# Causal attention in one kernel with a mixture of experts: attention steps without a loop, and scores in array tiles of 64 by 64

## The chip, the cores and the metric

The kernel runs on one core of a Trainium2 chip. The metric is the device time of one launch in microseconds; lower is better. The matrix engine (TensorE, here PE), VectorE (DVE), ScalarE (ACT) and GpSimd (POOL) work in parallel, each through a list of instructions of its own; SyncE (SP) issues the DMA transfers. They wait for one another through semaphores only. Matmul results go to PSUM, eight banks of 128 partitions by 512 float32.

## The reference

Input x has 16 sequences of 512 rows and 128 channels. What the change touches is the first half, causal attention with 16 heads of 8 channels on a normalised x:

```python
q = x @ wq_lat @ wq_heads
k = x @ wk_lat @ wk_heads
v = x @ wv_lat @ wv_heads
...
att = jnp.einsum('bhqd,bhkd->bhqk', q, k) * SCALE
causal = jnp.tril(jnp.ones((Tx, Tx), dtype=bool))
att = jnp.where(causal[None, None], att, -jnp.inf)
att = jax.nn.softmax(att, axis=-1)
y = jnp.einsum('bhqk,bhkd->bhqd', att, v)
...
return y @ w_proj + b_proj
```

Behind it stand a layer norm and a residual, a shared feed-forward block and twelve experts, of which each row uses two. The change does not touch those.

## The kernel before

The attention works through 64 quads; a quad is four heads of one sequence. Each engine runs `step(gs, g)` for gs = -2 to 65, and `quad_steps` (L383 to L398) calls it: steps -2 to 3 and 56 to 65 are written out, steps 4 to 55 are a loop of 13 iterations of four steps. Inside the loop a semaphore is compared with a register (L394 to L396), which needs register instructions ahead of the wait; where two semaphores are waited for, `wait_apart` (L68) makes the wait an instruction of its own, which counts a semaphore `passed` up.

For a quad the scores are computed twice. `scores_by_query` (L1226 on, `most` in the step) has queries on PSUM partitions; DVE reduces them to row maxima (L1664, five units per quad). The maxima are negated, split on POOL into three bfloat16 parts, turned on PE (`turn_maxima`, L1276), copied by ACT (L968, `mT_sb`) and sent by SP (L555) as three further rows under the queries in `quad_area`. `scores_by_key` (L1250 on, `by_key`) then has keys on partitions and contracts over 64 rows, maxima included, so that ACT can apply the exponential straight from PSUM (L948); POOL zeroes what lies above the diagonal (L721), and PE multiplies with the values (`products`, L1308, four heads in column tiles of 32). `project` (L1220) makes the next queries and keys in even steps, which ACT copies (L935, L936), POOL splits into bfloat16 parts, and SP stores and loads again (L510, L503).

Two quads' rows lie on partitions 0 to 63 and 64 to 127, so that each score matmul uses half the rows of the array and all 128 columns (64x128), and two, `rg` 0 and 1, run side by side into two banks. PSUM has a ring of three such pairs of banks (RING = 3): an item of a step waits in `wait_emptied` (L1181 on) for the emptying of the item three before. The order in which PE issues is written out by hand in its `step` (L1352 on). An even step is by_key 1, most 3, project, most 4, products 2, turn_maxima, by_key 4, most 0, by_key 2, products 1 and 3, by_key 0, most 1, by_key 3, products 0, most 2. An odd step is by_key 1, most 2, products 0, by_key 2, most 4, products 1, by_key 4, most 0, turn_maxima, products 3, by_key 3, most 3, products 2, most 1, by_key 0, turn_back. SP's step loads a quad (L503, four transfers) before it sends the maxima (L555).

Units 0 and 1 of `most` hold the blocks on the diagonal of four query tiles. There the mask is added by two matmuls per bank (L1238) ahead of the scores, one for each half of the queries; `mask_to` and `mask_of` are built once, by fourteen selects in a chain on POOL (L694 to L702).

Of the kernel before, what the change touches and what calls it, by code (L numbers as in the profile page):

```python
# [5 lines left out]
ALU = mybir.AluOpType  # L6
# [3 lines left out]
BF16 = mybir.dt.bfloat16  # L10
# [57 lines left out]
def wait_apart(engine, sem, value, passed):  # L68

    engine.wait_ge(sem, value)  # L70
    engine.sem_inc(passed, 1)
# [109 lines left out]
def build(nc, a, out):  # L181
    with ExitStack() as ctx:
# [11 lines left out]
        mask_to = sb("mask_to", [P, 2, P], BF16)  # L194
        mask_of = sb("mask_of", [P, 2, ROWS], BF16)
# [279 lines left out]
        def _(sp):  # L475
# [99 lines left out]
            quad_steps(sp, step)  # L575
# [74 lines left out]
        def _(pool):  # L650
# [171 lines left out]
            quad_steps(pool, step)  # L822
# [40 lines left out]
        def _(act):  # L863
# [147 lines left out]
            quad_steps(act, step)  # L1011
# [106 lines left out]
        def _(pe):  # L1118
# [62 lines left out]
            def wait_emptied(gs, g, at):  # L1181
# [24 lines left out]
                masks = items(gs)[at][0] == "max" and items(gs)[at][1] < 2  # L1206
# [4 lines left out]
                if masks:  # L1211
                    wait_apart(pe, ready, done, s_passed)
                else:
                    pe.wait_ge(ready, done)
# [7 lines left out]
            def scores_by_query(gs, g, u, bank):  # L1222

                slot = (gs + 2) % 4
                if nth(MAX_ORDER, gs, u) == 0:
                    wait_apart(pe, s_qk[slot], 16 * (g + 2 - slot) + 64, s_passed)  # L1226

                def score(rg, head, at, qt, keys, first, closes):
                    return pe.matmul(ps[:, bank + rg, at:at + keys], rows(2 * rg + head, 0, qt * P, qt * P + P, slot, ROWS - 3),  # L1229
                                     rows(2 * rg + head, 1, first, first + keys, slot, ROWS - 3), start=closes is None, stop=closes is not False)  # L1230

                if u < 2:
                    for half in range(2):
                        for rg in range(2):
                            row = slice(ROWS * rg, ROWS * rg + ROWS)
                            keys = ps[:, bank + rg, :].rearrange("p (j k) -> p j k", k=P)[:, :, ROWS * half:ROWS * half + ROWS]
                            of = mask_of[row, half:half + 1].broadcast_to([ROWS, NT, ROWS])
                            pe.matmul(keys, mask_to[row, half], of, start=(half == 0), stop=False)  # L1238
                    for j, qt in enumerate(DIAGONALS):
                        for rg in range(2):  # L1240
                            last = score(rg, u, j * P, qt, P, qt * P, j == NT - 1)
                elif u < 4:
                    for at, qt, keys in ((0, 1, P), (P, 3, 3 * P)):
                        for rg in range(2):
                            last = score(rg, u - 2, at, qt, keys, 0, None)
                else:
                    for head in range(2):
                        for rg in range(2):
                            last = score(rg, head, 2 * P * head, 2, 2 * P, 0, None)
                last.then_inc(s_mx, 1)  # L1250

            def scores_by_key(gs, g, n, bank):

                slot = gs % 4
                if nth(EXP_ORDER, gs, n) == 0:
                    pe.wait_ge(s_m[slot], 8 * (g - slot) + 32)
                places = (((0, 0, 0),), ((0, 1, 0), (0, 3, 384)), ((1, 0, 0),), ((1, 1, 0), (1, 3, 384)), ((0, 2, 0), (1, 2, 256)))[n]
                for head, kb, at in places:
                    w = T - kb * P
                    for rg in range(2):  # L1260
                        last = pe.matmul(ps[:, bank + rg, at:at + w], rows(2 * rg + head, 1, kb * P, kb * P + P, slot, ROWS),  # L1261
                                         rows(2 * rg + head, 0, kb * P, T, slot, ROWS), start=True, stop=True)
# [165 lines left out]
            quad_steps(pe, step)  # L1428
# [136 lines left out]
        def _(dve):  # L1565
# [384 lines left out]
            quad_steps(dve, step)  # L1950
# [121 lines left out]
```

## Time and profile before

| | before |
|---|---|
| median of 3 runs | 1133.36 us (1133.0 to 1135.47) |
| profiled execution | 1131.17 us |
| its span | 1129.3 us |
| mean granted clock | 0.953 of full speed |
| PE busy | 992.2 us, 88% of the span |
| DVE busy | 853.1 us, 76% |
| ACT busy | 722.5 us, 64% |
| POOL busy | 632.7 us, 56% |

The span is what the profiler saw between the first and the last instruction; the profiled execution's time also has what lies around it. Busy shares are means over stages: the attention with its start takes about the first half, the experts most of the rest. Matmul ends are modelled, and overlapping matmuls make PE look fuller than its array is. A line such as `ACT pT_area L948 <- PE ps L1261` in the view of the waits says that ACT's instruction of L948 sat idle until PE's of L1261 released it; in a timeline the same stands in brackets.

### The profile page before, as it was taken

How to read it: one execution, taken by the hardware profiler on the slowest of the kernel's cores; microseconds unless marked ns; L12 is line 12 of the kernel's file. 1: busy time of each engine (PE TensorE's matmuls, PEld its weight loads, DVE VectorE, ACT ScalarE, POOL GpSimd, SP SyncE). 2: the span in 40 equal slices, each digit the busy share in tenths (PEclk: the TensorE clock that was granted, in tenths of full speed). 3: DMA queues.
4: the chain of work that ended last, by engine and by line, in shares of the span. 5: the costliest groups of instructions: out<-in, count | busy, mean ns of one | idle time of the engine just before them, and what ended most of it. 6: DMA issues, size and time to landing. Idle time of an engine off the chain costs nothing. (4 is left out here: it accounts for less than half of the span.)

```text
span 1129.3 us, 31995 instructions
## 1 busy us (share of the span) xinstructions
PE 992.2 (88%) x8685; PEld 618.6 (55%) x8685; DVE 853.1 (76%) x2487; ACT 722.5 (64%) x1234; POOL 632.7 (56%) x1195
## 2 busy tenths in 40 slices
PE   4589999999999999978879998759999999998774
PEld 2553344443444434433456665339999888897532
DVE  5678888888888888877689985327777777777646
ACT  4578788888888888866646665316565555556426
POOL 4327777777777777755217777742444444444344
PEclk9889999999999999999959998969999999999988
DMA  8413333333333333343251111122222222221176
GB/s 221 104 31 104 112 104 109 113 106 106 105 107 113 113 110 104 107 115 103 74 214 57 54 54 56 51 80 60 61 66 67 60 65 67 63 61 57 32 252 197
DMA packets 135726, 108.21 MB, mean 96 GB/s; under 512 B 32207, under 2 KB 127866, under 8 KB 135658
## 3 DMA queue, kind: packets, MB, share of 16 engines
q1 hardware_dynamic: 124842, 88.19, 27.8%
q0 software_dynamic: 8544, 17.78, 4.4%
q10 hardware_dynamic: 2272, 1.45, 0.5%
q8 instruction: 28, 0.46, 0.2%
q14 instruction: 40, 0.33, 0.1%
HBM read 56.70 MB, written 50.68 MB: 95 GB/s over the span
## 5 line engine op out<-in xcount | busy, mean ns | idle before, releaser
L1664 DVE TENSOR_REDUCE maxima<-ps 128x8 f32<-128x1024 f32 x320 | 380.4, 1222 | 76.7 <-PE ps L1229 69.8
L948 ACT ACTIVATE pT_area<-ps 128x1024 f32<-128x1024 f32 x320 | 320.8, 1023 | 86.2 <-PE ps L1261 80.9
L843 POOL DMA_INDIRECT ys_dram<-quad_area,place_cur x139 | 133.1, 958 | 188.2 <-issue 126.5
L721 POOL TENSOR_SCALAR_AFFINE_SELECT pT_area<-pT_area 128x256 f32<-128x256 f32 (+1 forms) x448 | 186.6, 439 | 90.8 <-ACT pT_area L948 88.3
L1308 PE MATMUL ps<-pT_area,quad_area 128*32 128x512 f32 (+3 forms) x2048 | 185.5, 446 | 0.6 <-POOL pT_area L721 0.6
L833 POOL DMA_INDIRECT xs_dram<-quad_area,idx_cur x128 | 123.1, 961 | 74.6 <-issue 73.7
L1261 PE MATMUL ps<-quad_area 64*128 64x256 bf16 (+3 forms) x1024 | 125.9, 301 | 30.7 <-DMA quad_area<-mT_sb 28.1
L1991 DVE SCALAR_TENSOR_TENSOR quad_area<-ps,be_cur,xnT 128x256 f32<-128x256 f32 (+1 forms) x228 | 92.0, 456 | 61.5 <-PE ps L1541 28.0
L1530 PE MATMUL ps<-quad_area 128*128 128x256 f32 (+1 forms) x456 | 130.3, 368 | 7.0 <-DVE quad_area L1991 6.8
L1096 ACT ACTIVATE xnT<-ps,be_cur 128x256 f32<-128x256 f32 (+1 forms) x228 | 103.1, 453 | 49.2 <-PE ps L1531 48.1
L1229 PE MATMUL ps<-quad_area 61*128 61x128 bf16 (+2 forms) x1792 | 127.0, 241 | 4.7 <-ACT pT_area L948 2.7
L1531 PE MATMUL ps<-quad_area 128*128 128x256 f32 (+1 forms) x456 | 128.0, 362 | 0.0
L1541 PE MATMUL ps<-outT_area,quad_area 128*128 128x128 f32 x834 | 107.8, 278 | 2.7 <-DVE quad_area L2009 2.3
L1541 PEld LDWEIGHTS ps<-outT_area,quad_area 128*128 128x128 f32 x834 | 102.4, 192 | 10.8 <-issue 5.5
L1229 PEld LDWEIGHTS ps<-quad_area 61*128 61x128 bf16 x1792 | 70.1, 94 | 68.8 <-ACT pT_area L948 50.2
L1261 PEld LDWEIGHTS ps<-quad_area 64*128 64x128 bf16 x1024 | 38.4, 94 | 104.9 <-DVE maxima L1664 65.9
L1531 PEld LDWEIGHTS ps<-quad_area 128*128 128x128 f32 x456 | 84.2, 191 | 10.0
L1530 PEld LDWEIGHTS ps<-quad_area 128*128 128x128 f32 x456 | 78.5, 191 | 17.5 <-DVE quad_area L1991 11.0
L1085 ACT ACTIVATE quad_area<-ps 128x256 f32<-128x256 f32 (+1 forms) x76 | 27.7, 365 | 80.3 <-PE ps L1516 80.3
L1308 PEld LDWEIGHTS ps<-pT_area,quad_area 128*32 128x32 f32 x2048 | 43.7, 108 | 57.8 <-issue 48.0
L1081 ACT ACTIVATE quad_area<-pT_area 128x768 f32 x76 | 63.4, 835 | 0.1
L1238 PE MATMUL ps<-mask_of,mask_to 64*128 64x256 bf16 x512 | 50.8, 273 | 5.9 <-DVE maxima L1664 4.8
(234 smaller groups left out, 1501.9 us busy)
## 6 DMA issues: line engine op xcount, KB each, us to landing
qk_dram<-split_area SPq DMA_DIRECT2D x192, 128.0 KB, 2.3
quad_area<-qk_dram SPq DMA_DIRECT2D x256, 96.0 KB, 2.3
row_area<-xs_dram SPq DMA_DIRECT2D x63, 132.0 KB, 2.1
pT_area<-ys_dram SPq DMA_DIRECT2D x16, 512.0 KB, 5.0
pT_area<-in_L_ffn_We SPq DMA_DIRECT2D x12, 384.0 KB, 6.3
out_dram<-pT_area SPq DMA_DIRECT2D x7, 512.0 KB, 3.0
xs_dram<-row_area SPq DMA_DIRECT2D x5, 528.0 KB, 4.4
split_area<-in_L_ffn_We SPq DMA_DIRECT2D x12, 192.0 KB, 3.8
```

The lines of the kernel that those rows point to most:

```text
L721: return pool.affine_select(out=blocks, in_=blocks, compare_op=ALU.is_ge, fill=0.0, base=0, pattern=[[0, count], [1, P]], channel_multipli ...
L833: pool.indirect_dma_start(xs_dram, at, rows_cur[:, b % DEPTH, t, :], None).then_inc(s_scat[par], 16)
L843: pool.indirect_dma_start(ys_dram, at, ys[:, ns % 2, h, :], None).then_inc(s_yst[ns % 2], 16)
L948: act.activation(pT[:, gs % 2, n, :], ps[:, bank:bank + 2, :].rearrange("p a b -> p (a b)"), ACT.Exp).then_inc(s_exp, 1)
L1096: act.activation(gelE[:, ring, 0:width(ns)], ps[:, ring, 0:width(ns)], ACT.Gelu, bias=be_cur[:, ns % 8, 3 + k:4 + k]).then_inc(s_ge, 1)
L1229: return pe.matmul(ps[:, bank + rg, at:at + keys], rows(2 * rg + head, 0, qt * P, qt * P + P, slot, ROWS - 3), rows(2 * rg + head, 1, firs ...
L1261: last = pe.matmul(ps[:, bank + rg, at:at + w], rows(2 * rg + head, 1, kb * P, kb * P + P, slot, ROWS), rows(2 * rg + head, 0, kb * P, T, ...
L1308: last = pe.matmul(ps[32 * i:32 * i + 32, bank, kb * P:T], v_cur[:, slot, kb, i, :], pT[:, buf, n, 512 * rg + at:512 * rg + at + w], start ...
L1530: pe.matmul(ps[:, ring, 0:w], w1_cur[:, par, HR + k * P:HR + (k + 1) * P], xsT[:, par, 0:w], start=True, stop=True)
L1531: pe.matmul(ps[:, ring, RT:RT + w], w1_cur[:, par, k * P:(k + 1) * P], xsT[:, par, 0:w], start=True, stop=True).then_inc(s_he, 1)
L1541: last = pe.matmul(ps[:, Y_BANKS[par], h * C:(h + 1) * C], hidT[:, par, k, h * P:(h + 1) * P], w2_cur[:, par, k * C:(k + 1) * C], start=(k ...
L1664: dve.tensor_reduce(to, ps[:, bank:bank + 2, :].rearrange("p a (j k) -> p a j k", k=P), AX, ALU.max).then_inc(s_mxf, 1)
```

## The change

The change has four parts. `quad_steps` now calls every step from -2 to 65 with constants, so all 64 quads are written out on each engine, and `wait_apart` with a constant adds no count, so that the wait sits on the instruction behind it. All scores are computed in tiles of 64 rows by 64 columns: each matmul of 128 queries (or keys) becomes two of 64, which write partitions 0 to 63 and 64 to 127 of the same bank, so that four run where two ran. In units 0 and 1 one mask matmul per tile, after the scores, covers the later 64 keys of each block. The earlier 64 are all allowed, which needs another choice of keys: the first 64 queries of a tile take the 64 keys before their own block in place of the later half of it, and where there are none (the first tile) key 0 is scored 64 times. And POOL builds the smaller masks with four selects in place of fourteen.

```diff
 def wait_apart(engine, sem, value, passed):
     engine.wait_ge(sem, value)
-    engine.sem_inc(passed, 1)
+    if not isinstance(value, int):
+        engine.sem_inc(passed, 1)
...
-        def quad_steps(engine, step):
-            for g in range(FIRST, 4):
-                step(g, g)
-            with engine.Fori(1, B - EARLY) as it:
-                for q in range(4):
-                    step(4 + q, 4 * it + q)
-            for g in range(4 * (B - EARLY), LAST + 1):
+        def quad_steps(step):
+            for g in range(FIRST, LAST + 1):
                 step(g, g)
...
-                for half in range(2):
-                    same = to[:, half, ROWS * half:ROWS * half + ROWS]
-                    chain(pool.affine_select(out=same, in_=same, compare_op=ALU.not_equal, fill=1.0, base=0,
-                                             pattern=[[-1, ROWS]], channel_multiplier=1))
-                    chain(pool.affine_select(out=of[:, half], in_=of[:, half], compare_op=ALU.is_ge, fill=MASKED, base=0,
-                                             pattern=[[-1, ROWS]], channel_multiplier=1))
-                for late, value in ((to[:, 1, ROWS:], 0.0), (to[:, 1, 0:ROWS], 1.0), (of[:, 1], MASKED)):
-                    chain(pool.affine_select(out=late, in_=late, compare_op=ALU.not_equal, fill=value, base=1 - ROWS,
-                                             pattern=[[0, ROWS]], channel_multiplier=1))
+                chain(pool.affine_select(out=to, in_=to, compare_op=ALU.not_equal, fill=1.0, base=0,
+                                         pattern=[[-1, ROWS]], channel_multiplier=1))
+                chain(pool.affine_select(out=of[:, 0], in_=of[:, 0], compare_op=ALU.is_ge, fill=MASKED, base=0,
+                                         pattern=[[-1, ROWS]], channel_multiplier=1))
...
+                def half(rg, later, head, qt, at, keys, first, last=False):
+                    lo = qt * P + ROWS * later
+                    return pe.matmul(ps[ROWS * later:ROWS * later + ROWS, bank + rg, at:at + keys.shape[-1]],
+                                     rows(2 * rg + head, 0, lo, lo + ROWS, slot, ROWS - 3), keys, start=first, stop=last)
...
                 if u < 2:
-                    for half in range(2):
-                        for rg in range(2):
-                            row = slice(ROWS * rg, ROWS * rg + ROWS)
-                            keys = ps[:, bank + rg, :].rearrange("p (j k) -> p j k", k=P)[:, :, ROWS * half:ROWS * half + ROWS]
-                            of = mask_of[row, half:half + 1].broadcast_to([ROWS, NT, ROWS])
-                            pe.matmul(keys, mask_to[row, half], of, start=(half == 0), stop=False)
-                    for j, qt in enumerate(DIAGONALS):
-                        for rg in range(2):
-                            last = score(rg, u, j * P, qt, P, qt * P, j == NT - 1)
+                    for j, qt in enumerate(DIAGONALS):
+                        for rg in range(2):
+                            if qt == 0:
+                                half(rg, 0, u, qt, j * P + ROWS, key_rows(rg, u, 0, ROWS), True)
+                            else:
+                                half(rg, 0, u, qt, j * P, key_rows(rg, u, qt * P - ROWS, qt * P + ROWS), False)
+                        for rg in range(2):
+                            half(rg, 1, u, qt, j * P, key_rows(rg, u, qt * P, qt * P + P), qt == 0)
+                        if qt == 0:
+                            for rg in range(2):
+                                half(rg, 0, u, qt, j * P, key_rows(rg, u, 0, 1).broadcast_to([ROWS - 3, ROWS]), False)
+                    for later in range(2):
+                        for rg in range(2):
+                            row = slice(ROWS * rg, ROWS * rg + ROWS)
+                            late_keys = ps[ROWS * later:ROWS * later + ROWS, bank + rg, :].rearrange("p (j k) -> p j k", k=P)[:, :, ROWS:]
+                            last = pe.matmul(late_keys, mask_to[row], mask_of[row].broadcast_to([ROWS, NT, ROWS]), start=False, stop=True)
...
                     w = T - kb * P
-                    for rg in range(2):
-                        last = pe.matmul(ps[:, bank + rg, at:at + w], rows(2 * rg + head, 1, kb * P, kb * P + P, slot, ROWS),
-                                         rows(2 * rg + head, 0, kb * P, T, slot, ROWS), start=True, stop=True)
+                    for later in range(2):
+                        lo = kb * P + ROWS * later
+                        for rg in range(2):
+                            last = pe.matmul(ps[ROWS * later:ROWS * later + ROWS, bank + rg, at:at + w],
+                                             rows(2 * rg + head, 1, lo, lo + ROWS, slot, ROWS),
+                                             rows(2 * rg + head, 0, kb * P, T, slot, ROWS), start=True, stop=True)
```

The other units of `most` are split in the same way. The first place where the order of instructions moves is PE at the beginning of an even step (`by_key` 1, `most` 3, `project`, `most` 4, `products` 2). Before, inside the loop; the last figures of a row are the output's partitions and columns, or its shape:

```order
L1214 REGISTER_ALU
L1261 MATMUL ps<-quad_area 128x384 [waits m_loaded2,maxima_taken]
L1261 MATMUL ps<-quad_area 128x384
L1261 MATMUL ps<-quad_area 128x128 x2
L1214 REGISTER_ALU
L70 ISA [waits maxima_taken]
L1229 MATMUL ps<-quad_area 128x128 [waits qk_loaded0]
L1229 MATMUL ps<-quad_area 128x128
L1229 MATMUL ps<-quad_area 128x384 x2
L1220 MATMUL ps<-y_sb,w_qkv 128x512 [waits exp_done]
```

With the change (`by_key` is L1263, `most` L1217, `project` L1207):

```order
L1263 MATMUL ps<-quad_area 64x384 [waits m_loaded2,maxima_taken]
L1263 MATMUL ps<-quad_area 64x384 x3
L1263 MATMUL ps<-quad_area 64x128 x4
L1217 MATMUL ps<-quad_area 64x128 [waits qk_loaded0,maxima_taken]
L1217 MATMUL ps<-quad_area 64x128 x3
L1217 MATMUL ps<-quad_area 64x384 x4
L1207 MATMUL ps<-y_sb,w_qkv 128x512 [waits exp_done]
```

The three register and count instructions are gone, both waits of `most` sit on its first matmul, and each group has twice the matmuls. The second place is a unit with masks, in the same step (`most` 0, then `by_key` 2). Before:

```order
L1238 MATMUL ps<-mask_of,mask_to 128x4x64 [waits part1_ready]
L1238 MATMUL ps<-mask_of,mask_to 128x4x64 x3
L1229 MATMUL ps<-quad_area 128x128 x8
L1214 REGISTER_ALU
L1261 MATMUL ps<-quad_area 128x512 [waits maxima_taken]
L1261 MATMUL ps<-quad_area 128x512
```

With the change:

```order
L1217 MATMUL ps<-quad_area 64x64 [waits part1_ready]
L1217 MATMUL ps<-quad_area 64x64
L1217 MATMUL ps<-quad_area 64x128 x2
L1217 MATMUL ps<-quad_area 64x64 x2
L1217 MATMUL ps<-quad_area 64x128 x12
L1239 MATMUL ps<-mask_of,mask_to 64x4x64 x4
L1263 MATMUL ps<-quad_area 64x512 [waits maxima_taken]
L1263 MATMUL ps<-quad_area 64x512 x3
```

Twelve matmuls become 22, and the masks stand behind the scores. The third place is POOL's setup with the change, where before the pair of L696 and L698 stood four times and L701 six times ahead of the casts:

```order
L690 AFFINE_SELECT mask_to<-mask_to 64x64
L692 AFFINE_SELECT mask_of<-mask_of 64x64 [waits pool_step]
L690 AFFINE_SELECT mask_to<-mask_to 64x64 [waits pool_step]
L692 AFFINE_SELECT mask_of<-mask_of 64x64 [waits pool_step]
L694 CAST before_bf<-before 128x128 [waits pool_step]
L695 CAST ident_bf<-ident 128x128
L174 TENSOR_TENSOR pT_area<-pT_area,minus_half 128x8 [waits ln_root_steps] x2
```

The last row is the inverse root of the first normalisation (L173 before), which now has four selects ahead of it.

## Rows read from the trace of the kernel before

**Rows 1.** Window; busy us (count) of PE, PEld, DVE, ACT, POOL; clock, DMA share

```profile
100.00:450.00 350.00, 330.89 (x4163) 140.99 (x4159) 303.75 (x356) 282.57 (x356) 252.39 (x639) 1.00 0.38 108
```

**Rows 2.** Waits, 100 to 450 us: us in total, times, longest us

```profile
PE ps L1261 <- DMA quad_area<-mT_sb: 18.6, 24, 1.2
```

**Rows 3.** Timeline, PE, written-out steps: start us, duration us, line, operation, count [idle before]

```profile
83.89 0.24 PE L1276 MATMUL ps<-ident_bf,m_part 128*48 128x128 bf16 x1
...
87.53 0.39 PE L1261 MATMUL ps<-quad_area 64*128 64x384 bf16 x4 [1.17 <-DVE maxima L1664]
87.75 0.40 PE L1229 MATMUL ps<-quad_area 61*128 61x128 bf16 x4
88.07 1.12 PE L1220 MATMUL ps<-y_sb,w_qkv 128*128 128x512 f32 x2
...
90.02 0.24 PE L1276 MATMUL ps<-ident_bf,m_part 128*48 128x128 bf16 x1
...
98.23 0.24 PE L1276 MATMUL ps<-ident_bf,m_part 128*48 128x128 bf16 x1
```

**Rows 4.** The same view of PE, steps inside the loop

```profile
201.99 0.24 PE L1276 MATMUL ps<-ident_bf,m_part 128*48 128x128 bf16 x1
...
203.62 0.28 PE L1238 MATMUL ps<-mask_of,mask_to 64*128 64x256 bf16 x2
...
205.94 0.40 PE L1261 MATMUL ps<-quad_area 64*128 64x384 bf16 x4 [0.90 <-DMA quad_area<-mT_sb]
206.28 0.40 PE L1229 MATMUL ps<-quad_area 61*128 61x128 bf16 x4
...
208.55 0.24 PE L1276 MATMUL ps<-ident_bf,m_part 128*48 128x128 bf16 x1
...
216.83 0.24 PE L1276 MATMUL ps<-ident_bf,m_part 128*48 128x128 bf16 x1
...
223.10 0.24 PE L1276 MATMUL ps<-ident_bf,m_part 128*48 128x128 bf16 x1
...
231.54 0.24 PE L1276 MATMUL ps<-ident_bf,m_part 128*48 128x128 bf16 x1
```

**Rows 5.** The same view, ACT and then SP, same steps

```profile
201.61 1.02 ACT L948 ACTIVATE pT_area<-ps 128x1024 f32<-128x1024 f32 x1 [0.32 <-PE ps L1261]
202.53 0.26 ACT L968 ACTIVATE mT_sb<-ps 48x128 bf16<-48x128 bf16 x1
...
201.06 1.87 SPq L503 DMA_DIRECT2D quad_area<-qk_dram  x4
202.98 1.61 SPq L555 DMA_DIRECT2D quad_area<-mT_sb  x2
```

**Rows 6.** The same view of PE, an even step's unit with masks, and products

```profile
211.02 0.39 PE L1238 MATMUL ps<-mask_of,mask_to 64*128 64x256 bf16 x4
211.24 0.40 PE L1229 MATMUL ps<-quad_area 61*128 61x128 bf16 x8
211.46 0.40 PE L1261 MATMUL ps<-quad_area 64*128 64x384 bf16 x4
...
213.60 1.07 PE L1308 MATMUL ps<-pT_area,quad_area 128*32 128x512 f32 x8
```

**Rows 7.** Groups by form, weight loads, 100 to 450 us: busy us, mean ns

```profile
L1261 PEld LDWEIGHTS ps<-quad_area 64*128 64x128 bf16 x758 | 28.5, 94 | 70.2 <-DVE maxima L1664 47.5 <-DMA quad_area<-mT_sb 10.3 <-issue 9.3
```

**Rows 8.** Timeline of the start, POOL, then DVE

```profile
6.94 0.23 POOL L696 TENSOR_SCALAR_AFFINE_SELECT mask_to<-mask_to 64x64 bf16<-64x64 bf16 x1
...
11.70 0.24 POOL L701 TENSOR_SCALAR_AFFINE_SELECT mask_of<-mask_of 64x64 bf16<-64x64 bf16 x1
...
12.49 1.68 POOL L173 TENSOR_TENSOR pT_area<-pT_area,minus_half 128x8 f32<-128x8 f32 x1
...
14.21 0.17 DVE L1596 SCALAR_TENSOR_TENSOR pT_area<-pT_area 128x8 f32<-128x8 f32 x1 [6.63 <-POOL pT_area L173]
```

**Rows 9.** DMA queues, 80 to 135 us: packets, MB, share of 16 engines

```profile
q8 instruction: 6, 0.10, 0.8%
```

More of the change, by code:

```diff
@@ L193, in build @@
         ident_bf = sb("ident_bf", [P, P], BF16)
-        mask_to = sb("mask_to", [P, 2, P], BF16)
-        mask_of = sb("mask_of", [P, 2, ROWS], BF16)
+        mask_to = sb("mask_to", [P, ROWS], BF16)
+        mask_of = sb("mask_of", [P, 1, ROWS], BF16)
         ysum = kept_xT = y_sb
@@ L573, in step @@
                     store_late(4 * g + (EARLY - 1) * HEADS, 1, 2)
-            quad_steps(sp, step)
+            quad_steps(step)
             sp.wait_ge(s_st, 5 * QUADS)
@@ L820, in step @@
                     split_rows(gs, g, 2)
-            quad_steps(pool, step)
+            quad_steps(step)
             def scatter(ns, n):
@@ L1009, in copy_yT @@
                 act.activation(yT[:, ns % 2, :], ps[:, YT_TURN, :], ACT.Copy).then_inc(s_yTsb, 1)
-            quad_steps(act, step)
+            quad_steps(step)
             act.wait_ge(s_w2, 160)
@@ L1205, in wait_emptied @@
                 quad = g - back + AHEAD[kind]
-                masks = items(gs)[at][0] == "max" and items(gs)[at][1] < 2
                 if kind == "max":
@@ L1210, in wait_emptied @@
                     ready, done = s_exp, UNITS * quad + nth(EXP_ORDER, gs - back, u) + 1
[L1211 to L1214, printed above, removed]
+                wait_apart(pe, ready, done, s_passed)
             def project(gs, g, s, bank):
@@ new lines, in key_rows @@
+                def key_rows(rg, head, first, last):
+                    return rows(2 * rg + head, 1, first, last, slot, ROWS - 3)
+                if u < 2:
+                    for j, qt in enumerate(DIAGONALS):
[10 more added lines that the diff above has]
+                    for later in range(2):
@@ L1242, in scores_by_query @@
+                            last = pe.matmul(late_keys, mask_to[row], mask_of[row].broadcast_to([ROWS, NT, ROWS]), start=False, stop=True)
                 elif u < 4:
                     for at, qt, keys in ((0, 1, P), (P, 3, 3 * P)):
-                        for rg in range(2):
-                            last = score(rg, u - 2, at, qt, keys, 0, None)
+                        for later in range(2):
+                            for rg in range(2):
+                                last = half(rg, later, u - 2, qt, at, key_rows(rg, u - 2, 0, keys), True, True)
@@ L1246, in scores_by_query @@
                 else:
                     for head in range(2):
-                        for rg in range(2):
-                            last = score(rg, head, 2 * P * head, 2, 2 * P, 0, None)
+                        for later in range(2):
+                            for rg in range(2):
+                                last = half(rg, later, head, 2, 2 * P * head, key_rows(rg, head, 0, 2 * P), True, True)
                 last.then_inc(s_mx, 1)
@@ L1255, in scores_by_key @@
                 if nth(EXP_ORDER, gs, n) == 0:
-                    pe.wait_ge(s_m[slot], 8 * (g - slot) + 32)
+                    wait_apart(pe, s_m[slot], 8 * (g - slot) + 32, s_passed)
                 places = (((0, 0, 0),), ((0, 1, 0), (0, 3, 384)), ((1, 0, 0),), ((1, 1, 0), (1, 3, 384)), ((0, 2, 0), (1, 2, 256)))[n]
@@ L1259, in scores_by_key @@
                     w = T - kb * P
-                    for rg in range(2):
-                        last = pe.matmul(ps[:, bank + rg, at:at + w], rows(2 * rg + head, 1, kb * P, kb * P + P, slot, ROWS),
-                                         rows(2 * rg + head, 0, kb * P, T, slot, ROWS), start=True, stop=True)
+                    for later in range(2):
+                        lo = kb * P + ROWS * later
+                        for rg in range(2):
+                            last = pe.matmul(ps[ROWS * later:ROWS * later + ROWS, bank + rg, at:at + w],
+                                             rows(2 * rg + head, 1, lo, lo + ROWS, slot, ROWS),
+                                             rows(2 * rg + head, 0, kb * P, T, slot, ROWS), start=True, stop=True)
                 last.then_inc(s_st, 1)
@@ L1426, in project_y @@
                 last.then_inc(s_proj, 1)
-            quad_steps(pe, step)
+            quad_steps(step)
             pe.wait_ge(s_exp, UNITS * QUADS)
@@ L1948, in shared @@
                     tile_table()
-            quad_steps(dve, step)
+            quad_steps(step)
             dve.wait_ge(s_vcur, QUADS)
```

3 lines of the change are left out of this document (removed).

## Prediction, made before the changed kernel was run

> **What bounds the kernel now.** I read the windows first [rows 1]. In the steady part of the attention TensorE (PE) is busy for 330.89 us of 350, DVE for 303.75, ACT for 282.57, POOL for 252.39, all at a granted clock of 1.00, the 2.4 GHz level. PE is nearest to full, yet its busy share is inflated by overlapping matmuls, so I asked next for the waits [rows 2]: the reader is to see that PE waits at L1261 for the rows of maxima (`quad_area<-mT_sb`) 24 times, 18.6 us in all. The timeline gives the beat: in the looped steps the starts of `turn_maxima` (L1276) are 6.56, 8.28, 6.27 and 8.44 us apart [rows 4], so four quads take 29.55 us and two take 14.78; 350 / 14.78 = 23.7, one such wait per two quads, always at an even step. So each two quads are one loop: maxima turned on PE (201.99), copied by ACT (202.53), sent by SP (202.98), landed and first used by PE at 205.94 [rows 4, 5]; then the even step's scores, exponentials and maxima lead to the odd step's `turn_maxima`, after which it starts again. DVE needs at least 303.75 / 23.7 = 12.8 us per two quads, PE something over that; neither fills the 14.78. What counts is latency along this loop.
>
> **What leaving the loop gives.** `before` already holds written-out steps with constant waits: quads 2 to 4 stand 6.13 and 8.21 us apart (83.89, 90.02, 98.23), 14.34 for two [rows 3]. The same two places in the looped steps (201.99, 208.55, 216.83) take 14.84 [rows 4]. So constants are worth 0.50 here. It can be seen where: the first scores by key to the next group is 205.94 to 206.28, 0.34 us, in the loop, and 87.53 to 87.75, 0.22, written out, because separate register and count instructions stood between; and from `turn_maxima` to those scores it is 3.95 against 3.64. For the other two places (6.27 + 8.44 = 14.71 looped [rows 4]) no undisturbed written-out row exists. At least nothing is gained there, at most they also fall to 14.34, 0.37. I take 0.25, nearer the upper end, since the 8.44 contains a delay of SP's that partly stays: four loads of L503 from 201.06 on, after waits, stand ahead of the L555 that sends the maxima [rows 5], and the change leaves that order as it is. Per iteration 0.50 + 0.25 = 0.75; 13 iterations give **-9.8 us** (bounds -6.5 and -11.3). The six written-out pairs of steps gain nothing from this.
>
> **What the shorter masks give.** A mask and its scores in one unit take 211.02 to 211.46, 0.44 us, half for the four masks, half for the eight scores [rows 6]. Each row half streams 2 x 256 mask columns and 4 x 128 score columns, 1,024. Now each of four tiles streams 512 score columns and 256 of mask, 768, a quarter less: 0.11 us, if the four run side by side. Two units per quad, 128 in all, would make 14.1 us. But only what lies on the loop counts. The odd step's two are covered: behind the one (203.62) PE waits 0.90 us at 205.94 in any case [rows 4], and an earlier end of the other, just ahead of the turn at 201.99, helps nobody, since ACT cannot copy the turned maxima before its exponential begun at 201.61 ends, at 202.53 [rows 5]. Of the even step's two I count one, so 0.11 x 32 pairs = **-3.5 us** (bounds 0 and -14.1).
>
> **What tiles of 64 by 64 cost.** The number of score matmuls and masks per quad goes from 52 to 100, and of weight loads as well. The trace of before has no tile of 64 by 64. The nearest rows are the products of L1308: eight matmuls in column tiles of 32, 512 columns each, take 1.07 us from 213.60 on [rows 6], while two matmuls of 512 columns in the same type over the whole array take 1.12 [rows 3]. So four column tiles do run side by side, and eight weight loads cost nothing in view: bound below, 0. The upper bound: a load of a score group takes 94 ns [rows 7]; if each group's two further loads stood wholly in view, that is 0.19 us, on some six groups of the loop per pair, 0.19 x 6 x 32 = +36 us. I take 0.02 per group, close to the products' nothing, because only the first four loads of a group have no matmul of their own shape to hide behind: 0.02 x 6 x 32 = **+3.8 us**. The Trainium skill ("TensorEngine Tiling (Array Packing)", Restrictions and Instruction Overhead) speaks against the change: column tiling switches its fast weight load off, and each matmul costs some 60 cycles whatever its width. By that rule a unit of 22 matmuls would take, as an estimate, 22 x 25 ns = 0.55 us and not 0.33, and the sum would be about 7 us higher. The products' rows, column-tiled and not slowed by their loads, do not bear the first half out; no row here decides the second.
>
> **What the shorter setup gives.** Fourteen chained selects run on POOL from 6.94 to the casts; the first inverse root (L173) starts behind them at 12.49, and DVE idles 6.63 us until 14.21 for it [rows 8], with the whole normalisation behind. Ten selects go. The chain from 6.94 to the last select at 11.70 is thirteen steps, 0.37 each, so ten are 3.7 us. DVE would still wait 2.9 us, so its own work does not take over. I take **-3.7 us** (bounds 0, if the loads of x or weights are late next, and -3.8).
>
> **Instruction fetch.** Between 80 and 135 us, half of it written out, the instruction queue moved 6 packets [rows 9]. Written out throughout, the attention fetches them all along; its cover is that the DMA engines are a little over a third busy (0.38, [rows 1]). I cost it at nothing; without cover it is a rival.
>
> **Sum.** -9.8 - 3.5 + 3.8 - 3.7 = -13.2. The profiled execution took 1131.17; 1118.0 comes out. The median of the runs is 1133.36, 2.2 higher, so I predict 1120.2 us.
>
> **Rivals.**
> *PE itself is the bound*, and every mask saving counts. For it: 330.89 of 350 busy [rows 1]. Against: the 18.6 us of waits for transfers [rows 2], which no busy engine would have. All four units of a pair then count, -14.1 in place of -3.5, and the time is about 1110.
> *Another wait takes over.* When PE comes sooner, the ring of three pairs of banks, DVE at 12.8 us per pair, or SP's queue sets the beat. For it: DVE's busy share, and SP's loads ahead of L555 [rows 5]. Then half the loop's saving stays and masks and tiles matter no more; -3.7 - 4.9 leaves about 1125.
> *Slower: small tiles pay per instruction.* A unit of 12 matmuls takes 0.44 us now [rows 6], 0.037 each. If that were a price per instruction and not of the columns, 22 cost 0.81, +0.37 on the one unit of the loop, and the other five groups of eight cost 0.29, some 0.05 more than the narrow ones now: +0.37 + 0.25 = 0.62 per pair, 32 pairs +20 in place of -3.5 + 3.8, and the time is about 1140. Its place is the score groups of the even step; it makes the kernel slower than before from 0.42 us per pair on, where it eats the other 13.5 (9.8 + 3.7). The rule of the skill's page on tiling named above is this mechanism in a milder form; by its 0.55 us the time stays below before's.
> *The change does nothing*, since fetched instructions delay the maxima's transfers as much as the constants save: 16 KB packets on the engine that carries a row of maxima, 0.4 us per pair in the mean. For it: the 6 packets in 55 us [rows 9]. Against: those very steps ran at 14.34 per pair [rows 3]. Then about 1131 to 1134.
>
> **How the numbers follow.** Forecast 0.60, PE bound 0.14, another wait 0.12, slower tiles 0.09, nothing 0.05. The forecast's own range, from the bounds of the terms (loop -6.5 to -11.3, masks 0 to -7, tiles 0 to +8), is 1112 to 1127. The range that holds 8 in 10 takes in both faster rivals: 1108 to 1130. A measurement of this kernel can tell some 0.2%, 2.3 us, from no change. Faster by more: 0.60 + 0.14 + 0.12 = 0.86; slower 0.09; the same 0.05.
>
> **What would show it.** Right: starts of `turn_maxima` 14.2 to 14.4 us apart per two quads in all steps; scores after the first group by key 0.22 behind it; a mask group followed by the next unit 0.33 to 0.36 after its first score; the first inverse root at 8.7 us; a wait for `mT_sb` still once per pair. Wrong: a unit of over 0.44 us, weight loads on the timeline between tiles of a group, the pair's beat at 14.7 or above, or more than one instruction packet near each late transfer.

## Result and profile after

The changed kernel took 1116.3 us (median of 4 runs, 1115.21 to 1117.18), the kernel before 1134.34 beside it. The ratio is 0.9848 with a 95% interval of 0.983 to 0.9865, 17.2 us less (the two medians differ by 18.0). The forecast was 1120.2 in a range of 1108 to 1130. The profiled execution took 1117.18 us, its span 1115.4, 13.9 less than before's. Runs of one kernel scatter by several microseconds, and the granted clock goes with it in the main: of 30 further runs of the kernel before, the three with a mean granted clock of 0.956 took 1127.7 to 1128.7 us and the three with 0.946 took 1135.7 to 1139.1, though the one with 0.957 took 1134.2.

The windows of the steady attention, with the columns of [rows 1]:

```profile
100.00:450.00 350.00, 330.96 (x6597) 144.34 (x6595) 310.05 (x363) 291.51 (x366) 258.39 (x654) 1.00 0.41 114
```

PE has 6,597 matmuls in place of 4,163 and is busy for the same 331 us; DVE and ACT do 2 to 3% more in the same stretch, which is the progress. The waits of PE for the maxima, and of ACT for PE, in the same stretch:

```profile
ACT pT_area L939 <- PE ps L1263: 48.6, 121, 1.2
...
PE ps L1263 <- DVE maxima L1667: 14.6, 19, 0.8
...
PE ps L1263 <- DMA quad_area<-mT_sb: 4.4, 5, 1.3
```

The wait at the even step's first group is still there once per two quads ([rows 2]: 24 times, 18.6 us; now 19 + 5 times, 19.0 us), only that most are now put down to DVE's reductions, which end at nearly the same moment. The timeline of PE over two quads, to be held beside [rows 4] and [rows 6], then SP and DVE:

```profile
196.06 0.24 PE L1279 MATMUL ps<-ident_bf,m_part 128*48 128x128 bf16 x1
...
199.94 0.41 PE L1263 MATMUL ps<-quad_area 64*64 64x384 bf16 x8 [0.77 <-DVE maxima L1667]
200.16 0.42 PE L1217 MATMUL ps<-quad_area 61*64 61x128 bf16 x8
200.50 1.12 PE L1207 MATMUL ps<-y_sb,w_qkv 128*128 128x512 f32 x2
201.56 0.41 PE L1217 MATMUL ps<-quad_area 61*64 61x256 bf16 x8
201.90 0.64 PE L1311 MATMUL ps<-pT_area,quad_area 128*32 128x256 f32 x8
202.47 0.24 PE L1279 MATMUL ps<-ident_bf,m_part 128*48 128x128 bf16 x1
...
204.88 0.40 PE L1217 MATMUL ps<-quad_area 61*64 61x64 bf16 x18
205.12 0.28 PE L1239 MATMUL ps<-mask_of,mask_to 64*64 64x256 bf16 x4
205.23 0.38 PE L1263 MATMUL ps<-quad_area 64*64 64x384 bf16 x8
...
210.46 0.24 PE L1279 MATMUL ps<-ident_bf,m_part 128*48 128x128 bf16 x1
...
197.05 1.57 SPq L551 DMA_DIRECT2D quad_area<-mT_sb  x2
...
195.20 4.61 DVE L1667 TENSOR_REDUCE maxima<-ps 128x8 f32<-128x1024 f32 x4
```

The turns of the maxima stand 6.41 and 7.99 us apart, 14.40 for two quads in place of 14.71 and 14.84. The first score group is followed after 0.22 (0.34 in the loop before). A unit with masks now takes 204.88 to 205.23, 0.35 us and not 0.44, so four tiles do run side by side. But a group of eight small matmuls ahead of another shape takes 0.34 (200.16 to 200.50, 201.56 to 201.90), where four wide ones took 0.32 (87.75 to 88.07 [rows 3]). The rows of SP and DVE show what the wait is for: DVE's reductions end at 199.81, and PE's group starts at 199.94, 1.32 us after SP has issued both transfers of the maxima (198.62). Before it was 1.35 after them (204.59 to 205.94 [rows 4, 5]), so the transfer still comes last, by about 0.1 us; experiment 4 tests this.

The start, POOL and DVE, as in [rows 8]:

```profile
6.71 0.23 POOL L690 TENSOR_SCALAR_AFFINE_SELECT mask_to<-mask_to 64x64 bf16<-64x64 bf16 x1
...
8.63 1.68 POOL L174 TENSOR_TENSOR pT_area<-pT_area,minus_half 128x8 f32<-128x8 f32 x1
...
10.35 0.17 DVE L1599 SCALAR_TENSOR_TENSOR pT_area<-pT_area 128x8 f32<-128x8 f32 x1 [2.62 <-POOL pT_area L174]
```

The inverse root is 3.86 us earlier, and DVE waits 2.62 in place of 6.63. The larger of the two instruction queues moved 86 packets of 16 KB in the whole span, against 28.

Between the turns of quads 4 and 56, which holds the former loop, the two traces differ by 9.4 us (98.23 to 482.75, now 95.12 to 470.28). Of the other 4.5 us by which the spans differ, 3.1 lie ahead of quad 4's turn and 3.4 in the experts, while the end of the attention and the shared block behind it take 3.1 us longer; the last stage gives back 1.1. The gain in the experts has no term in the forecast.

### The profile page after: what moved, and what is told of

The parts are those of the page before. It is cut to its first block, busy times and chain, and to the rows that moved or that the text cites. A ratio compares the mean times of both kernels' runs of the same rounds, so it can differ in the third digit from the quotient of the medians.

```text
span 1115.4 us, 34300 instructions
## 1 busy us (share of the span) xinstructions
PE 985.2 (88%) x11757; PEld 619.1 (56%) x11757; DVE 851.2 (76%) x2487; ACT 722.9 (65%) x1234; POOL 630.8 (57%) x1185
## 4 chain that ended last, share of the span: by engine, by line
PE 24%; DMA 7%; DVE 7%; POOL 6%; issue 5%; DVEq 1%; ACT 1%; ACTq 1%; SPq 0%; POOLq 0%
POOL xs_dram L824 6%; DMA ys_dram<-quad_area,place_cur 5%; PE ps L1533 5%; PE ps L1534 5%; PE ps L1544 5%; PE ps L1559 1%; DMA xs_dram<-quad_area,idx_cur 1%; PE ps L1519 1%; DVEq L1988 1%; PE ps L1443 1%; PE ps L1562 1%; PE ps L1427 1%; PE ps L1563 1%; PE ps L1441 1%; PE ps L1565 1%
## 5 line engine op out<-in xcount | busy, mean ns | idle before, releaser
L1263 PE MATMUL ps<-quad_area 64*64 64x384 bf16 (+3 forms) x2048 | 130.6, 309 | 30.8 <-DVE maxima L1667 17.3
L1217 PE MATMUL ps<-quad_area 61*64 61x128 bf16 (+3 forms) x3840 | 131.4, 240 | 11.0 <-DVE maxima L1667 6.4
L1217 PEld LDWEIGHTS ps<-quad_area 61*64 61x64 bf16 x3840 | 71.2, 107 | 93.4 <-ACT pT_area L939 62.3
L1263 PEld LDWEIGHTS ps<-quad_area 64*64 64x64 bf16 x2048 | 46.5, 105 | 107.2 <-DVE maxima L1667 81.0
L1443 PE MATMUL ps<-y_sb,ws 128*128 128x512 f32 x64 | 39.8, 709 | 14.9 <-DVE v_all L1822 14.7
```

What stands on the lines that cost most here:

```text
L1217: return pe.matmul(ps[ROWS * later:ROWS * later + ROWS, bank + rg, at:at + keys.shape[-1]], rows(2 * rg + head, 0, lo, lo + ROWS, slot, RO ...
L1263: last = pe.matmul(ps[ROWS * later:ROWS * later + ROWS, bank + rg, at:at + w], rows(2 * rg + head, 1, lo, lo + ROWS, slot, ROWS), rows(2 * ...
```

## Experiments

Each was a variant of the kernel before or of the changed one. What is compared is the time, and in the trace the beat, the distance of the starts of `turn_maxima` over two quads. It is given as the median of the 26 pairs between quads 4 and 56 (as the mean where the loop is kept, since its two places differ). In the four traces that have the changed kernel's attention it is 14.40 to within 0.002 us, so it tells a tenth of a microsecond that the time alone can't.

**1. Only written out.** The kernel before with two edits: old tiles, masks and setup.

```diff
-    engine.sem_inc(passed, 1)
+    if not isinstance(value, int):
+        engine.sem_inc(passed, 1)
...
-            with engine.Fori(1, B - EARLY) as it:
...
+            for g in range(FIRST, LAST + 1):
                 step(g, g)
```

> The kernel before with all steps written out and nothing else: old tiles, old masks, old setup. Theory (the beat of two quads is a loop of waits, and register waits lengthen it): turn_maxima 14.3 to 14.5 us apart per two quads in all steps, from 14.78; 9 to 11 us faster than before, about 1123 to 1125. Rival (matrix engine full, so the gain is the masks' and tiles'): 14.6 to 14.8, at most 3 us faster.

Measured: 1114.52 us (1110.74 to 1116.46), ratio 0.9811 (0.9788 to 0.9833). PE's turns:

```profile
193.94 0.24 PE L1272 MATMUL ps<-ident_bf,m_part 128*48 128x128 bf16 x1
...
200.22 0.24 PE L1272 MATMUL ps<-ident_bf,m_part 128*48 128x128 bf16 x1
...
208.30 0.24 PE L1272 MATMUL ps<-ident_bf,m_part 128*48 128x128 bf16 x1
```

6.28 and 8.08 here, and 14.334 for two quads over all: the theory's beat, and below the changed kernel's 14.40. So the whole gain of the loop comes from writing it out, and tiles and masks together take 0.07 per two quads back. The written-out steps of before, at 14.34, still had the counts of `wait_apart`, and experiment 1 has none; so on this loop the counts cost nothing that can be seen, and the register waits, or whatever else the loop form brings, cost all of it. The time, though, is some 9 us below the theory's 1123 to 1125. In this one trace 4.6 us are gained ahead of quad 4's turn, although the old setup is still there, and 4.1 in the experts (experiments 9 and 10, and the last section).

**2. Ten selects put back** into the changed kernel's setup.

```diff
+                for _ in range(5):
+                    chain(pool.affine_select(out=to, in_=to, compare_op=ALU.not_equal, fill=1.0, base=0,
+                                             pattern=[[-1, ROWS]], channel_multiplier=1))
```

> The changed kernel with ten redundant selects put back into the setup's chain. Theory: the first inverse root at 12.4 us in place of 8.6, the first turn_maxima 2.7 to 3.8 us later, the beat untouched at 14.40, the time 2.7 to 3.8 us over the changed kernel's (about 1119 to 1120). Rival (the start waits for loads anyway): the first turn_maxima under 1 us later, 1116 to 1117.

Measured: 1119.52 us (1117.93 to 1120.74), 3.2 over the changed kernel; beat 14.40; the inverse root at 12.82. DVE's first reduction of maxima came at 48.37, against 45.01 in the changed kernel and 48.10 in the kernel before. The shorter setup is worth 3.1 to 3.4 us at this place and 3.2 in the time, as the theory has it; experiment 8 does not bear it out.

**3. Wide tiles but for the masked units**, in the changed kernel.

```diff
-                        for later in range(2):
-                            for rg in range(2):
-                                last = half(rg, later, u - 2, qt, at, key_rows(rg, u - 2, 0, keys), True, True)
+                        for rg in range(2):
+                            last = whole(rg, u - 2, at, qt, keys)
...
```

> The changed kernel with 64 by 64 tiles in the units with masks only; the other scores in tiles of 64 by 128 as before. Theory (a group of small tiles costs some 0.02 us more): the beat falls from 14.40 to about 14.3, 2 to 4 us faster than the changed kernel. Rival A (small tiles pay per matmul): 14.1 or less, 10 us or more faster. Rival B (small tiles are free, a change of tile shape costs): 14.4 to 14.6, the same time or up to 6 us slower.

Measured: 1121.57 us (1118.4 to 1123.18), beat 14.57. Rival B holds. PE around a masked unit:

```profile
204.34 0.39 PE L1263 MATMUL ps<-quad_area 64*128 64x512 bf16 x2
204.66 0.42 PE L1217 MATMUL ps<-quad_area 61*64 61x64 bf16 x18
204.91 0.28 PE L1243 MATMUL ps<-mask_of,mask_to 64*64 64x256 bf16 x4
205.12 0.39 PE L1263 MATMUL ps<-quad_area 64*128 64x384 bf16 x4
...
205.44 1.06 PE L1310 MATMUL ps<-pT_area,quad_area 128*32 128x512 f32 x8
```

The wide group is followed by the small one after 0.32, where a group of one shape follows after 0.22 to 0.24, and the unit takes 0.46 in place of 0.35: about 0.1 us at each change of tile shape. Small tiles in the masks alone therefore lose: the beat is 14.57, for 14.334 with wide tiles and the old masks (experiment 1) and 14.40 with small tiles in all scores.

**4. The odd step's turn earlier**, in the changed kernel.

```diff
+                    copy_max_rows(gs, g)
                     probabilities(gs, g, 4)
-                    copy_max_rows(gs, g)
...
+                    turn_maxima(gs, g)
                     by_key(gs, g, 4)
                     most(gs, g, 0)
-                    turn_maxima(gs, g)
```

> The changed kernel with odd steps' turn_maxima two groups earlier on TensorE (ahead of by_key 4 and most 0) and its copy ahead of ScalarE's exponential 4. Theory (the beat runs through that copy, which stands behind exponential 4): the transfer starts about 1 us earlier, and the beat falls by 0.2 to 0.3, to where DVE's reductions of the odd step free the banks: 14.1 to 14.2, 6 to 9 us faster than the changed kernel. Rival (TensorE or DVE is full, the wait for the maxima only follows): 14.4, no faster.

Measured: 1115.89 us (1111.36 to 1119.45), beat 14.30. PE, then DVE:

```profile
197.38 0.41 PE L1263 MATMUL ps<-quad_area 64*64 64x384 bf16 x8 [0.15 <-DMA quad_area<-mT_sb]
197.86 0.41 PE L1217 MATMUL ps<-quad_area 61*64 61x128 bf16 x8
...
193.00 4.81 DVE L1667 TENSOR_REDUCE maxima<-ps 128x8 f32<-128x1024 f32 x4
```

PE's wait for the maxima falls from 0.77 to 0.15, and the next group now stands 0.48 behind it in place of 0.22: it waits for DVE's four reductions, which end at 197.8. So the transfer was on the loop, by 0.10 us; behind it stands DVE. The direction is the theory's, the size is a third to a half of it, and in the time nothing of it can be seen: 1115.89 for 1116.3, where the theory had 6 to 9 us.

**5. The changed kernel again**, without an edit.

> The changed kernel once more, beside the next three. All theories: 1114 to 1118 us, turn_maxima 14.40 us apart per two quads; its waits for late maxima of over 1 us, one or two in the attention, need not fall on the same quads (if they come from fetched instructions, they may; if by chance, they won't).

Measured: 1116.19 us (1112.58 to 1117.55), ratio 0.9841 (0.9818 to 0.9863); beat 14.40. The change's first trace has one turn late by 0.57 (quad 43), this one turns late by 0.07 and 0.12 on other quads. What makes them late stays open: in the first, one packet of each of the two instruction queues moved during the wait, but in experiment 11 a turn was 1.1 late with no instruction packet near it.

**6 and 7. More masks.** In the changed kernel the mask products of a unit are issued more than once; 6 doubles them in all steps, 7 triples them in even ones.

```diff
+                    times = 2 if gs >= 0 else 1
+                    for again in range(times):
+                        for later in range(2):
...
+                                last = pe.matmul(late_keys, mask_to[row], mask_of[row].broadcast_to([ROWS, NT, ROWS]), start=False, stop=again == times - 1)
```

> The changed kernel with each mask product of the steps 0 on issued twice, so that a unit streams as many columns per tile as before the change (masked scores are then lower still; the probabilities are the same). Theory after the first four runs (all four units of two quads lie behind ScalarE's exponentials or the maxima's copy, so the shorter masks gave nothing): the beat stays at 14.40 to 14.42, the time within 1 us of the changed kernel. Rival A (one unit per two quads counts, as the forecast had it): 14.51, 3.5 us slower. Rival B (TensorE is full): 14.83, 14 us slower.

> The changed kernel with the mask products of even steps issued three times, 0.21 us more in each of the two units. Theory (these units have 0.2 to 0.4 us of slack against ScalarE's four exponentials in a row): the beat 14.40 to 14.50. Rival A (one of the two units counts in full): 14.61. Rival B (both count): 14.82.

Measured: 6 took 1119.82 us (1116.25 to 1121.42), 7 1127.61 in a single run. Turns of 6, then of 7:

```profile
195.23 0.24 PE L1281 MATMUL ps<-ident_bf,m_part 128*48 128x128 bf16 x1
...
201.53 0.24 PE L1281 MATMUL ps<-ident_bf,m_part 128*48 128x128 bf16 x1
...
209.69 0.24 PE L1281 MATMUL ps<-ident_bf,m_part 128*48 128x128 bf16 x1
```

```profile
198.61 0.24 PE L1281 MATMUL ps<-ident_bf,m_part 128*48 128x128 bf16 x1
...
205.01 0.24 PE L1281 MATMUL ps<-ident_bf,m_part 128*48 128x128 bf16 x1
...
213.29 0.24 PE L1281 MATMUL ps<-ident_bf,m_part 128*48 128x128 bf16 x1
```

14.46 and 14.68 here, 14.468 and 14.686 over all. Both theories missed. One reading fits both runs: the even step's two units lie one behind the other ahead of ACT's exponentials, with some 0.14 us of slack together, so that 0.21 more costs 0.07 and 0.43 more costs 0.29. What the slack is against was not tried by itself. The kernel of run 6 streams as many columns per tile as before the change; so the shorter masks are worth 14.468 - 14.400 = 0.068 per two quads, 2.2 us over 32 pairs, and small tiles with the old amount of columns are 14.468 - 14.334 = 0.134 above run 1, 4.3 us.

**8. Old tiles, the earlier turn, and the selects behind the second inverse root**, all on top of experiment 1.

```diff
                 inverse_root(pool, rstd1[:, tiles], root1[:, 0, tiles], minus_half).then_inc(s_pow1, 1)
+                if k == 1:
+                    build_masks()
```

> All steps written out with the old tiles and masks (the first run), and two things more: odd steps' turn_maxima and its copy earlier, and the fourteen selects behind the second inverse root. Theory (constants and setup are worth their time, tiles nothing): the beat 14.20 to 14.25, the first inverse root at about 7.5 us, 1108 to 1111 us, faster than every other version. Rival (with the old tiles the earlier turn gives nothing, since DVE ends last): 14.33, 1110 to 1114.

Measured: 1113.65 us (1112.5 to 1117.48), ratio 0.9829 (0.9806 to 0.9851); beat 14.31, inverse root at 7.91, first reduction at 45.14. The rival's beat, nearly: with old tiles DVE ends as late as the transfer. Its time can't be told from experiment 1's, and hardly from the changed kernel's; the 1108 to 1111 us of the theory were missed. DVE's first reduction comes 2.7 us earlier than in experiment 1 (47.84), and the time has 0.9 of it.

**9 and 10. The counts in the experts.** 9 is the kernel before with the new `wait_apart` alone. 10 is the changed kernel with the old, counting wait in the experts' steps (on DVE, POOL and SP).

```diff
-                    wait_apart(dve, s_yst[ns % 2], stored(ns - 8, n - 8), s_passed)
+                    wait_counted(dve, s_yst[ns % 2], stored(ns - 8, n - 8), s_passed)
...
-                wait_apart(dve, s_b2c, n + 1, s_passed)
-                wait_apart(dve, s_wt, 4 * n + 4, s_passed)
+                wait_counted(dve, s_b2c, n + 1, s_passed)
+                wait_counted(dve, s_wt, 4 * n + 4, s_passed)
...
```

> The kernel before with the new wait_apart alone (constants are not counted); loop, tiles, masks and setup as before. Theory (the experts' written-out last steps, where each count stands ahead of a DVE instruction, are a gain that the forecast overlooked): looped quads at 14.78 per two as before; the experts' stage, first row turn to first sum, 306 us in place of 310; 4 to 5 us faster than before. Rival (the 310 us of before's trace was chance): the stage as before or scattered, the time within 1.5 us of before's.

> The changed kernel with the old, counting wait in the experts' steps (DVE, POOL and SP) only. Theory: the stage takes 310 us again, 4 us slower than the changed kernel, about 1120; the attention's beat 14.40. Rival: 306 and 1116.

Measured: 9 took 1124.08 us (1122.97 to 1125.51), ratio 0.9916 (0.9888 to 0.9945), beat 14.78. 10 took 1119.68 us (1118.62 to 1121.69), 3.4 over the changed kernel, beat 14.40. From the first row turn of the experts to the first sum it is 310.1 us before, 304.6 in 9, 308.9 in 10, and 306.7 and 305.7 in the changed kernel's two traces. DVE in the last, written-out expert steps, before the change:

```profile
1045.31 0.21 DVE L1971 SCALAR_TENSOR_TENSOR weight_other<-row_area,be_cur 128x1 f32<-128x1 f32 x1
1045.67 0.16 DVE L1974 TENSOR_TENSOR weight_cur<-weight_cur,weight_other 128x1 f32<-128x1 f32 x1
1046.40 0.87 DVE L1991 SCALAR_TENSOR_TENSOR quad_area<-ps,be_cur,xnT 128x128 f32<-128x128 f32 x3 [0.57 <-issue]
...
1049.57 0.87 DVE L1991 SCALAR_TENSOR_TENSOR quad_area<-ps,be_cur,xnT 128x128 f32<-128x128 f32 x3 [0.57 <-issue]
```

The same of 9:

```profile
1041.92 0.21 DVE L1972 SCALAR_TENSOR_TENSOR weight_other<-row_area,be_cur 128x1 f32<-128x1 f32 x1
1042.16 0.16 DVE L1975 TENSOR_TENSOR weight_cur<-weight_cur,weight_other 128x1 f32<-128x1 f32 x1
1042.88 0.87 DVE L1992 SCALAR_TENSOR_TENSOR quad_area<-ps,be_cur,xnT 128x128 f32<-128x128 f32 x3 [0.56 <-PE ps L1542]
...
1045.82 0.87 DVE L1992 SCALAR_TENSOR_TENSOR quad_area<-ps,be_cur,xnT 128x128 f32<-128x128 f32 x3 [0.56 <-PE ps L1542]
```

And of 10:

```profile
1040.51 0.21 DVE L1980 SCALAR_TENSOR_TENSOR weight_other<-row_area,be_cur 128x1 f32<-128x1 f32 x1
1040.87 0.16 DVE L1983 TENSOR_TENSOR weight_cur<-weight_cur,weight_other 128x1 f32<-128x1 f32 x1
1041.60 0.87 DVE L2000 SCALAR_TENSOR_TENSOR quad_area<-ps,be_cur,xnT 128x128 f32<-128x128 f32 x3 [0.57 <-issue]
```

From `weight_other` to the sum that waits for it it is 0.36 with the count and 0.24 without, 0.12 each, twice per step (the second place is the product behind the sum with the bias); a step takes 3.17 with and 2.94 without. Over the last twelve steps, from one `weight_cur` sum to the next, it is 39.1 us before and 38.8 in 10, against 36.1 in 9 and 35.9 in both traces of the changed kernel: 2.9 us either way. This is shown from both sides, by undoing and by doing it alone. The 5.5 us of the stage in 9 is more than these steps explain, and of the 9.8 us of its median the stage is little more than half (its profiled execution, 1125.51, is 5.7 below before's). The rest stays open, beside a scatter of before's runs of several microseconds. The shared block between attention and experts calls `wait_apart` too (L1898, L1903), in steps that were written out already; from the last turn to the first row turn it takes 218.4 us before and 217.7 to 220.3 in the other traces, so nothing can be seen of its counts.

**11. The odd step's masks three times.** The edit is that of 7, for odd steps in place of even ones.

> The changed kernel with the mask products of odd steps issued three times, 0.21 us more in each of these two units. Theory (these units lie behind the maxima's copy and the transfer): the beat 14.40 to 14.45. Rival (TensorE is full): 14.83.

Measured: 1119.52 us in a single run; the turns, 14.40 for two quads although these units stream 0.43 us more:

```profile
197.21 0.24 PE L1281 MATMUL ps<-ident_bf,m_part 128*48 128x128 bf16 x1
...
203.40 0.24 PE L1281 MATMUL ps<-ident_bf,m_part 128*48 128x128 bf16 x1
...
211.61 0.24 PE L1281 MATMUL ps<-ident_bf,m_part 128*48 128x128 bf16 x1
```

So PE is not the bound, and the odd step's units are covered.

## Why the prediction was right, and where it was not

The sum of -13.2 us was meant for five terms and came near the measured 17.2; its parts stand so. That it came so near is in part luck: a missed term and a loop term taken too small (together 5.4 us) stand against three terms that were too favourable (2.4 us).

- *What bounds the kernel.* Right: a loop of waits, not a full engine. Experiment 11 gives PE 0.43 us more work per two quads and the beat stays; experiment 4 sends the maxima earlier and the beat falls.
- *Leaving the loop, -9.8.* Right in kind and short, by more than its bound of -11.3 allows. Experiment 1 has 14.334 per two quads, the value of the written-out steps that the trace of before already held (14.34 [rows 3]); over the 26 pairs between quads 4 and 56 that is 372.7 us for 384.5, -11.8. Of the "register and count instructions" to which the prediction put the 0.50, the counts have no part: those written-out steps had them. The step that was too careful is the second pair of places, 0.25 taken for the 8.44: it fell to 8.08, so SP's loads ahead of the transfer did not hold it.
- *Shorter masks, -3.5.* Right that the odd units count for nothing (11). The even step's two count together behind 0.14 us of slack, so the term is -2.2 (6 and 7), not one whole unit.
- *Tiles of 64 by 64, +3.8.* Right in size: +4.3, 0.134 per two quads (6 against 1), with some 0.02 us per group ahead of another shape (0.34 for 0.32). The 0.02 was picked between 0 and 0.19, near the end to which the products pointed, so that it fits so closely is luck; its reason, loads with no matmul to hide behind, was not tried. The weight loads grew from 94 ns [rows 7] to between 104 and 107. The rival of a price per instruction fell: a unit of 22 matmuls takes 0.35 us, and the rival had 0.81. With it fell the estimate of 0.55 us that the prediction drew from the Trainium skill, page "TensorEngine Tiling (Array Packing)" (Instruction Overhead): the overhead of some 60 cycles that the page states for each matmul does not add up over matmuls in different tiles. No run here shows what one such matmul alone takes.
- *Shorter setup, -3.7.* Nearly right: DVE's first reduction is 3.1 us earlier (45.01 for 48.10), and putting the selects back costs 3.2 us of time (2). But taking them out of the way of the old tiles left 0.9 us of time (8 against 1), so it is shown from one side only.
- *Instruction fetch, 0.* Right as far as it can be seen: experiment 1 has the beat of the few steps that were written out before. Single late transfers remain, under 1 us in all in the changed kernel.
- *What was missed.* The forecast took `wait_apart` for a matter of the attention. It is used in the experts too, whose first and last steps were written out already; there the count goes, which shortens the last twelve steps by 2.9 us, and to undo it costs 3.4 us of time (9 and 10). So the sentence ahead of the prediction that the change does not touch the experts is wrong. No rival had this. Of the rivals, only "another wait takes over" had some truth: DVE stands 0.1 us behind the transfer (4, 8), but it took nothing from the constants.
- *The range.* The bounds that the prediction names for its own range give 1111 to 1131, not 1112 to 1127 (at the slow end -6.5 + 0 + 8 - 3.7 = -2.2), and those of masks and tiles are narrower there than in their paragraphs, with no reason given. The wider range of 1108 to 1130 holds either way.

With the measured sizes: -11.8 - 2.2 + 4.3 - 3.1 - 3.4 = -16.2, against 17.2 (15.3 to 19.3 by the interval of the ratio). This leans on the 3.4 of experiment 10; with the 9.8 of experiment 9 it would be -22.6. Nor does experiment 1 add up: it is 20.2 us faster than before, and its two terms make 15.2. So the terms from beats are firm, those from times hold to some 5 us, and what makes up those 5 us stays open.

The half of the change that looked like the idea, small tiles with fewer mask columns, costs about 2 us net in the attention and pays only by the four selects in place of fourteen; experiment 1 without it is as fast within the scatter (1114.52 for 1116.3, at a mean granted clock of 0.952 to 0.956 for 0.946 to 0.952).

## What to carry to other kernels

Before a loop is unrolled or a helper of it touched, look for steps that are already written out: their beat is what the change will give, already measured, and 14.34 was it here to a hundredth. Then list every caller of a helper that is edited; the calls in another stage gave a fifth of this gain. And before columns are saved on an engine that seems full, ask which unit has slack behind it: two of four here were covered, and the other two shared 0.14 us.

## What the runs showed of the hardware

- A change of tile shape between groups on PE (64 by 128 to 64 by 64 and back) takes about 0.1 us (experiment 3). The trace of before had this price already: two groups of 512 columns per row half are followed after 0.22 us by a group of their own shape and after 0.32 by one of another (87.53, 87.75, 88.07 [rows 3]).
- A wait that is an instruction of its own with a count delays the DVE instruction after it by 0.11 to 0.12 us, against the same wait carried by that instruction (experiments 9 and 10). On PE no such delay shows: the written-out steps of before had the count, and their next group still stands 0.22 behind (87.53 to 87.75 [rows 3]).
- In all thirteen traces PE, DVE and ACT stand still together once, for 1.5 to 4.4 us between 50 and 58 us, with nothing in the profile that they could wait for. DVE's wait and a window behind it, before, in the changed kernel and in experiment 1 (`remote` stands where nothing on record released the wait; the granted clock is the last figure but two of a window):

```profile
DVE maxima L1664 <- remote: 4.5, 1, 4.5
...
60.00:64.00 4.00, 4.00 (x23) 3.37 (x22) 2.41 (x6) 2.32 (x5) 0.20 (x1) 0.55 0.00 0
```

```profile
DVE maxima L1667 <- remote: 5.8, 1, 5.8
...
56.00:60.00 4.00, 4.00 (x41) 3.12 (x30) 1.96 (x5) 2.08 (x6) 0.00 (x0) 0.50 0.00 0
```

```profile
DVE maxima L1660 <- remote: 3.2, 1, 3.2
...
56.00:60.00 4.00, 3.40 (x28) 2.86 (x28) 3.21 (x6) 3.60 (x8) 0.06 (x1) 1.00 0.00 0
```

In the first two PE stood idle for 4.2 and 5.4 us, and the granted clock is then at its 1.2 GHz level for a while; in experiment 1 PE stood idle for 2.3 us, and the clock stays at the 2.4 GHz level. None of this has a visible tie to any edit, and the start of the attention scatters by more than the setup's 3 us: quad 4's turn stands at 98.23 before, at 95.12 in the changed kernel, and at 93.59 in experiment 1, which has the old setup. The cause was not tried.
